# Two tiles of the next chunk loaded into scratch, and the constants loaded from another queue

## What is computed

```python
h = _layernorm(x) @ W.T + bias
x = x + block_cumsum_flat(h)         # running sum over blocks of 1024 flat elements: along each row
y = _layernorm(x)
h = silu((y @ w1.T) * s1) * ((y @ w2.T) * s2)      # 1024 -> 4096
h = gelu((h @ h1.T) * sh1)                         # 4096 -> 4096
h = gelu((h @ h2.T) * sh2)                         # 4096 -> 4096
x = x + (h @ w3.T) * s3                            # 4096 -> 1024
```

## Time and profile before

| | us |
|---|---|
| runs of the kernel before (2) | 2632.32 and 2653.05, median 2642.68 |
| the profiled execution | 2637.21 |
| its span, slowest core (2) | 2635.7 |
| spans of the eight cores | 2610.3 to 2635.7 |
| TensorE busy (core 2) | 2536.6 |
| VectorE, ScalarE, GpSimd busy | 211.6, 286.9, 273.3 |

### The profile page before, as it was taken

The page is one execution under the profiler, slowest core; times in us unless marked ns, Lnnn a source line. Parts: engine busy times, 40 slices in busy tenths (PEclk is TensorE's granted clock), DMA queues, the critical chain, the costliest instruction groups (busy, mean ns, idle before and its releaser), DMA issues.

```text
span 2635.7 us, 25250 instructions; the slowest of 8 cores (2610.3 to 2635.7 us)
## 1 busy us (share of the span) xinstructions
PE 2536.6 (96%) x11474; PEld 1147.6 (44%) x11708; DVE 211.6 (8%) x222; ACT 286.9 (11%) x258; POOL 273.3 (10%) x184
## 2 busy tenths in 40 slices
PE   5899999999999999999978999899999999999999
PEld 1344444444444444444433444344444444444444
DVE  3511100000000000000154111000000000000000
ACT  3311110000000000000032111000000000000000
POOL 0000111111111111111000001111111111111110
PEclk9999999999999999999989999999999999999999
DMA  7264799998889888998933457999988998999983
GB/s 137 37 85 64 72 76 74 83 80 72 77 76 80 76 73 77 79 80 96 149 75 48 64 83 72 75 77 79 77 74 76 78 77 75 76 76 79 81 92 68
DMA packets 635434, 207.30 MB, mean 79 GB/s; under 512 B 594368, under 2 KB 631232, under 8 KB 635328
## 3 DMA queue, kind: packets, MB, share of 16 engines
q0 software_dynamic: 629568, 188.76, 77.4%
q1 hardware_dynamic: 5760, 16.92, 2.1%
HBM read 386.02 MB, written 8.39 MB: 150 GB/s over the span
## 4 chain that ended last, share of the span: by engine, by line
PE 86%; DMA 9%; DVE 2%; issue 1%; another core or an unknown queue 1%; ACT 0%; SPq 0%; POOL 0%; DVEq 0%; ACTq 0%; POOLq 0%
PE ps L193 85%; DMA wb<-h1T 5%; DMA x_sb<-xT 3%; DMA outT<-x_sb 2%; DVE u_sb L269 1%; DVE x_sb L545 0%; PE ps L385 0%; PE ps L396 0%; SPq L316 0%; DVE stat L255 0%; DVE stat L367 0%; DVE stat L275 0%; ACT v_sb L374 0%; SPq L202 0%
## 5 line engine op out<-in xcount | busy, mean ns | idle before, releaser
L193 PE MATMUL ps<-v_sb,wb 128*128 128x512 bf16 x6021 | 1325.0, 380 | 19.3 <-DVE v_sb L294 12.9
L193 PE MATMUL ps<-u_sb,wb 128*128 128x512 bf16 x5268 | 1164.1, 380 | 23.5 <-DMA wb<-h1T 17.7
L193 PEld LDWEIGHTS ps<-v_sb,wb 128*128 128x128 bf16 x6144 | 602.0, 98 | 742.1 <-issue 20.3
L193 PEld LDWEIGHTS ps<-u_sb,wb 128*128 128x128 bf16 x5376 | 527.0, 98 | 657.6 <-issue 27.7
L153 POOL DMA_DIRECT2D wb<-h1T x64 | 107.3, 1676 | 801.1 <-PE ps L193 687.8
L153 POOL DMA_DIRECT2D wb<-h2T x64 | 107.2, 1676 | 776.8 <-PE ps L193 752.5
L545 DVE SCALAR_TENSOR_TENSOR x_sb<-ps,s_sb,x_sb 128x1024 f32<-128x1024 f32 x16 | 20.5, 1281 | 1905.0 <-PE ps L193 1905.0
L522 ACT ACTIVATE u_sb<-ps,sh_sb 128x1024 bf16<-128x1024 f32 x64 | 71.3, 1114 | 812.8 <-PE ps L193 774.7
L502 ACT ACTIVATE v_sb<-ps,sh_sb 128x1024 bf16<-128x1024 f32 x64 | 71.3, 1114 | 809.0 <-PE ps L193 783.3
L477 DVE SCALAR_TENSOR_TENSOR u_sb<-ps,s_sb,v_sb 128x1024 bf16<-128x1024 f32 x64 | 82.1, 1283 | 359.9 <-PE ps L193 337.4
L470 ACT ACTIVATE v_sb<-ps,s_sb 128x1024 bf16<-128x1024 f32 x64 | 71.3, 1115 | 356.7 <-PE ps L193 345.1
(11 more groups left out here) (29 smaller groups left out, 111.6 us busy)
## 6 DMA issues: line engine op xcount, KB each, us to landing
wb<-h1T POOLq DMA_DIRECT2D x64, 1024.0 KB, 15.8
wb<-h2T POOLq DMA_DIRECT2D x64, 1024.0 KB, 15.1
wb<-w1T POOLq DMA_DIRECT2D x16, 1024.0 KB, 10.6
wb<-w2T POOLq DMA_DIRECT2D x16, 1024.0 KB, 15.3
wb<-w3T POOLq DMA_DIRECT2D x16, 1024.0 KB, 11.6
x_sb<-xT SPq DMA_DIRECT2D x16, 512.0 KB, 9.5
outT<-x_sb SPq DMA_DIRECT2D x16, 512.0 KB, 4.7
wb<-wT POOLq DMA_DIRECT2D x4, 1024.0 KB, 12.1
```

The costliest lines, as they stand in the source:

```text
L193: return e.matmul(out, lhs, rhs, start=st, stop=sp)
```

## The change

The eight loads of constants are issued by ScalarE ("scalar") and no longer by SP ("sync"). In the first chunk, after the instructions of h2 and ahead of those of w3, ScalarE issues two new loads: tiles 6 and 7 of the next chunk's x into stat_m and stat_msq. They wait until layer norm 2 of the first chunk is over on VectorE and ScalarE, and each has a semaphore of its own. The casts and squares of tiles 6 and 7 for the next chunk read these copies. The reloads of tiles 6 and 7 into x_t stay as they are, since x_t is what the attention result is added to; that addition (xadd) now waits for the load of its tile as well.

```diff
-            consts_evt = plan.add("sync", dma_to(dst, src), inc=s_cst, inc_n=16)
+            consts_evt = plan.add("scalar", dma_to(dst, src), inc=s_cst, inc_n=16)
...
-                xadd_evt[o] = plan.add("vector", fadd, waits=[evY], inc=s_ve)
+                xadd_evt[o] = plan.add("vector", fadd,
+                                       waits=[evY, xl_evt[o]], inc=s_ve)
...
+            ln2_ve_end = (s_ve, s_ve.n)
+            ln2_sc_end = (s_sc, s_sc.n)
...
+            ex_evt = [None, None]
             if cidx + 1 < NCH:
...
+                c1e = (cidx + 1) * C
+                for t_, dst_ in ((6, stat_m), (7, stat_msq)):
+                    def fex(e, t_=t_, dst_=dst_, c1e=c1e):
+                        return e.dma_start(out=dst_,
+                                           in_=xT[t_ * P:(t_ + 1) * P, c1e:c1e + C])
+                    ex_evt[t_ - 6] = plan.add("scalar", fex,
+                                              waits=[ln2_ve_end, ln2_sc_end],
+                                              inc=s_ex[t_ - 6], inc_n=16)
...
-                    def fc3(e, o=o):
-                        return e.tensor_copy(vre(XBF, o), x_t(o))
+                    xsrc = x_t(o) if o < 6 else (stat_m if o == 6 else stat_msq)
+                    src_rdy = ([next_pre["xl"][o]] if o < 6 else [ex_evt[o - 6]])
+                    def fc3(e, o=o, xsrc=xsrc):
+                        return e.tensor_copy(vre(XBF, o), xsrc)
                     next_pre["xbf"][o] = plan.add(
                         "vector", fc3,
-                        waits=[next_pre["xl"][o], ln2_stats_end], inc=s_ve)
-                    def fs3(e, o=o):
-                        return e.activation(vre(X2, o), x_t(o), AF.Square)
+                        waits=src_rdy + [ln2_stats_end], inc=s_ve)
+                    def fs3(e, o=o, xsrc=xsrc):
+                        return e.activation(vre(X2, o), xsrc, AF.Square)
                     next_pre["x2"][o] = plan.add(
                         "scalar", fs3,
-                        waits=[next_pre["xl"][o], ln2_stats_end], inc=s_sc)
+                        waits=src_rdy + [ln2_stats_end], inc=s_sc)
```

More of the change, by code:

```diff
@@ L93, in build_nc @@
         h_st = [ec(nc.semaphore("s_st%d" % i)) for i in range(ND)]
+        h_ex = [ec(nc.semaphore("s_ex%d" % i)) for i in range(2)]
         h_w = [ec(nc.semaphore("s_w%d" % q)) for q in range(4)]
@@ L104, in build_nc @@
         s_st = [Sem(h) for h in h_st]
+        s_ex = [Sem(h) for h in h_ex]
         XN, XBF, X2, HA = 0, ND * C, 2 * ND * C, 3 * ND * C
@@ L436, in build_nc @@
             attn_end_pe = (s_pe, s_pe.n)
-            xn2_evt, _, _ = ln_phase(lambda i: [xadd_evt[i]],
+            xn2_evt, rstd2_evt, msq2_evt = ln_phase(lambda i: [xadd_evt[i]],
                                      war_xbf_x2=attn_end_pe,
```

## The result

The changed kernel takes 0.9894 of the time of the kernel before (95% interval 0.9865 to 0.9924), about 28 us less, with 20 to 36 us inside the interval. The median over all runs is 2625.76 us (25 runs) against 2653.88 (24 runs). In some executions the cores of one die run at a lower clock and take longer; the ratios, and the core medians further down, leave these out. The profiled execution took 2613.88 us, where 2613.0 had been forecast.

What follows compares the result with a forecast made beforehand. The prediction took matmuls (85% of the chain) as the bound, so transfers pay only where TensorE waits. From the profiled 2637.21 us it took 10.0 (start) and 14.2 (seam), giving 2613.0, range 2598 to 2634.

Steps and rivals of the forecast that it cites:

- Place of the gains: Only the kernel's start and the seam between the two column chunks would change, no other place.
- a gain of 10.0: Start: with queues taking turns, the last x tile ends near 26.8 us and L255 comes 10.0 us earlier.
- the cover: Start: constants land about 21 us, leaving TensorE time for tiles 0 to 6's fourteen sum matmuls before x ends near 27.
- some 250 before: Start: of the constants' 1152 packets, some 250 would have moved by 3 us.
- take until about 21: Start: the constants' remaining 904 packets, at 51 per us beside x, would be through at about 21 us.
- L255 at 33.0, gain 5.9: Start: constants come with the last x tile, all sixteen sum matmuls follow; 25% together with issue time only.
- issue time only: Start: shared DMA engines let x end only 4.5 us earlier, total 2618.5; 25% together with constants landing with x.
- Seam: Between chunks: all sixteen sum matmuls run through, L255 3.79 us after the first, gain 14.2 us.
- what could make it wrong: Seam: a late store or reload of tile 5 pushes fw3(6) past the last w3 matmul (7.5 us slack).
- I take nothing: Seam: TensorE idles about 3.5 us before the triangular matmul, clock assumed to hold, cost 0; clock fall given 8%.
- The bound of 3.0: Seam: if the clock falls after the idle time, the price is at most 3.0 us, kept for the range.
- Sum: Whole kernel: 2637.21 us less 10.0 at the start and 14.2 at the seam gives 2613.0.

Runs made afterwards that it cites:

- Splitting the wait: Changed kernel with the matrix of ones on its own semaphore, so the sum matmuls wait for it alone: ratio 0.9895, fastest core 2588.0 us.
- the two kernels with the gap filled: A third attention group ahead of the first triangular step, in the changed kernel (ratio 0.9936) and, given back mid-loop, in Start mended and three tiles (0.9911).
- constants-only kernel: Kernel before with one edit, the eight constants issued by ScalarE: ratio 0.9971, fastest core 2606.6 us.
- Start mended and three tiles: Changed kernel with ones on its own semaphore, the other seven constants behind x on SP, tile 5 copied too: ratio 0.9913, fastest core 2587.8 us.
- the lag at the front: Start mended and three tiles with three attention groups ahead of the first triangular step, lag given back mid-loop: ratio 0.9911, fastest core 2585.6 us.

## Why the prediction came out as it did

- *Place of the gains*: right. The stretches between start and seam did not move (1273.78 and 1273.76 us on core 1).
- *Start, x*: "a gain of 10.0" failed by 2.3 us; the last cast came 7.7 us earlier in the mean. About half of this is the price of the constants' packets. I had charged them by the time they occupy the DMA engines, 0.8 us of delay, and they cost x 2.0 (constants beside x or behind it: 29.5 and 27.5 us over the profiles). The rest lies at the end: x's rate was near the 51 per us of the forecast, but the 214 packets still to come at 22 us (mean of the cores) took about 8 us, where 51 per us gives 4.2. Why was not found. (Some 30 of the 904 packets that I called small constants were x's first, with 0.12 of the 0.21 MB.)
- *Start, the cover*: "some 250 before" and "take until about 21" failed. The 250 packets were those that SP's queue had passed by 3 us with nothing beside it; on ScalarE's queue, beside x, 5 had passed by then in the mean of the cores (274 before). The constants so started level with x, with as many packets, 1152, and passed one for one with it (569 and 569 from 12 to 24 us), so they ended with it: the bias landed at 31.8 on core 0, the last x tile was cast at 31.75. The case was in the text as a rival (L255 at 33.0, gain 5.9), but with x's end still at 26.8. With both, the gain of L255 was 3.2 us in the mean, 1.6 from slowest core to slowest core. Splitting the wait gives 4.6 us back.
- *The rival "issue time only"* gave 2618.5 for a start gain of 4.5. Its size is near the truth, but its mechanism isn't: x alone gained more than its 4.48 us of earlier issue, and TensorE lost it again by waiting. The Trainium skill's rule in "DMA: Bandwidth & Descriptors", Rules for kernel authors, says that spreading DMAs over queues brings no bandwidth and only saves issue time. For the total the trace agrees: the last weight tile of the start landed at 51.0 us after and at 48.7 before. The order in which the data arrives changed all the same; with the constants behind x its last tile came 10.1 us earlier.
- *Seam*: right where nothing else is late. 3.79 us from first sum matmul to L257 on six cores, 14.2 us by the forecast's own count; for the eight cores the mean went from 19.5 to 4.2. That tile 5 would be the next to be late, noted as what could make it wrong, happened on two cores for 1.2 and 2.0 us.
- *The clock at the seam*: "I take nothing" failed. Idle was 3.42 us, as forecast (3.5), and then the clock fell on every core: 1.7 us on seven of them, 1.3 on core 0. The bound of 3.0 held it. In the two kernels with the gap filled the first pair and the group behind it run at full speed on all 16 cores, so the idle time caused it. Its length alone does not decide: in the ten profiles with the new seam and this gap, 74 of 79 cores lose the clock and five do not, and one core of the constants-only kernel lost it after 2.18 us.
- *Sum*: 16.8 us on core 1, where the forecast had 24.2. What brought the profiled execution to 2613.88 is 10.3 us less in the long stretches on the slowest core: its waits for h1T were 6.1 us shorter (17.7 before, 11.6 after), and behind fewer waits it lost some 4 us less. The forecast held the waits constant, put their movement only into the range, and had no term for what they cost beyond their length. Start, seam and clock together gave 13.3 us on the slowest core, 10.9 less than forecast, and that 10.3 came back from elsewhere is luck.

**What stays open.** The first comparison gave 0.9894, two others of the same kernel 0.9922 and 0.9927. The slowest core lies above the fastest by 27.2 us in the kernel before and 18.6 in the changed one in one comparison (medians over the runs), and by 16.8 and 15.8 in another; in a third, on the chip of the first, the kernel before alone shows 13.9. Whether the change shortens the waits for h1T a little, or these are two samples of the same scatter, the runs do not decide. Nor was anything tried on h1T's loads, so why they come late is not shown, and what limited x's stream once constants and weights were out of its way was not found.

**The best version.** Start mended and three tiles, with or without the lag at the front, has fastest cores 4.8 and 7.0 us below the changed kernel, and ratios of 0.9913 and 0.9911 to the kernel before. Against the changed kernel, 0.9927, that is no difference the intervals can tell.

## What to carry to other kernels

When transfers are spread over queues, what counted here was how many packets each queue holds, more than how many bytes, and which wait needs the last of them: give the one small operand that is needed first a semaphore of its own, and put the others behind the large load. A load that returns into the tile it has just left can be taken off the path with a copy in idle scratch, and the next tile in line is then the one to check. When a stall goes, check how long the matmul engine idles in the chain behind it, since the shorter work before it makes that idle longer. And when a forecast of the slowest of several cores comes out right, compare a core without chance waits, piece by piece, before believing the steps.

## What the runs showed of the hardware

- From 12 to 24 us three queues passed 569, 567 and 569 packets, one for one, with 2.07, 0.58 and 0.06 MB. The constants, 0.14 MB in 1152 packets, so needed 24.6 us for the last to land beside x and the weights, where it had been 9.4; seven of them, 0.11 MB, delayed the 4.19 MB of x by 2.0 us (seven profiles against three).
- Loads issued by ScalarE appear as a hardware queue of their own, q10. Its issues lengthened from 0.41 us to 2.79 for the last; before, SP's had reached 0.87.
- TensorE at 2.4 GHz, then idle 3.4 us, went on at 1.2 GHz on all eight cores of the changed kernel's profile, at once (pairs of 1.01 us) or within the next group (5.17 us where 3.61 is full speed), and on 74 of 79 cores in ten such profiles. It cost 1.3 to 1.7 us where it fell once. After 2.56 us of idle it had not fallen, in other runs after 2.18 and 1.98 us it had.
- A wait of 8.47 us for a weight tile made its stage 11.0 us longer, and the clock was low behind it: the mean granted clock on that core was 0.50 from 1660 to 1663 us, 0.76 to 1670 and 1.00 after that.
